# Experts of a mixture: outputs turned back later, rows turned earlier, biases copied first

## The reference

```python
x = x + gnn(layernorm(x), adj, adj, ...)     # two products with adj matrices per batch, gates, relu
x = x + ffn(layernorm(x), Wg, bg, W1, b1, W2, b2)

def ffn(x, Wg, bg, W1, b1, W2, b2):          # D = 128, H = 512, E = 8
    gate_logits = xf @ Wg + bg
    top_w, top_i = jax.lax.top_k(gate_logits, 2)
    w_dense = sum(one_hot(top_i, E) * softmax(top_w)[..., None], axis=1)
    for e in range(E):
        h = gelu(xf @ W1[e] + b1[e])
        out = out + w_dense[:, e:e+1] * (h @ W2[e] + b2[e])
```

## Time and profile before

| what | us |
|---|---|
| median of 3 runs (lowest, highest) | 772.68 (769.83, 773.42) |
| the profiled execution | 766.71 |
| its span, first to last instruction | 764.9 |
| PE busy | 689.8 |
| DVE busy | 625.5 |
| ACT busy | 515.6 |
| POOL busy | 501.9 |

### The profile page before, as it was taken

One profiled execution on the slowest core, in us unless ns is written; L12 is line 12 of the kernel. 1 busy time (PEld: TensorE's weight loads), 2 busy tenths in 40 slices (PEclk: granted clock), 3 DMA queues, 4 the chain that ended last, 5 costly groups with the idle time before them and its releaser, 6 DMA issues.

```text
span 764.9 us, 18892 instructions
## 1 busy us (share of the span) xinstructions
PE 689.8 (90%) x5004; PEld 627.9 (82%) x5004; DVE 625.5 (82%) x2129; ACT 515.6 (67%) x1389; POOL 501.9 (66%) x460
## 2 busy tenths in 40 slices
PE   3879999799997549999998999999999999999991
PEld 2557677577675439999998999998999999999990
DVE  5989986889989648888888788887888888888881
ACT  3888878478875326676776677776677777777770
POOL 1534656365665774655678578886888888888883
PEclk9997977578887559999999999999999999999996
DMA  8465878463522266578857867459764543544310
GB/s 255 145 203 159 287 261 97 80 140 106 208 92 76 98 189 187 180 216 285 254 169 242 258 176 192 129 173 359 225 170 127 140 126 99 152 124 126 86 43 15
DMA packets 100336, 127.07 MB, mean 166 GB/s; under 512 B 37367, under 2 KB 61824, under 8 KB 100240
## 3 DMA queue, kind: packets, MB, share of 16 engines
q1 hardware_dynamic: 81600, 83.41, 39.4%
q0 software_dynamic: 17344, 42.51, 16.6%
q10 hardware_dynamic: 1296, 0.14, 0.2%
HBM read 71.41 MB, written 56.99 MB: 168 GB/s over the span
## 4 chain that ended last, share of the span: by engine, by line
PE 50%; DMA 4%; issue 1%; POOL 1%; SPq 0%; POOLq 0%; DVE 0%
PE bank L1262 7%; PE bank L1264 7%; PE bank L1263 7%; PE bank L1276 7%; PE bank L1277 7%; PE bank L1281 7%; DMA w_t<-w_split 4%; PE bank L1290 3%; PE bank L1252 3%; POOL out_dram L645 1%; SPq L482 0%; POOLq L151 0%; SPq L466 0%; DVE row L1137 0%; SPq L476 0%
## 5 line engine op out<-in xcount | busy, mean ns | idle before, releaser
L767 ACT ACTIVATE act_f<-bank,b_t 128x256 f32<-128x256 f32 x560 | 220.0, 476 | 42.6 <-PE bank L1264 41.8
L645 POOL DMA_INDIRECT out_dram<-row,to_row x140 | 182.0, 1300 | 47.6 <-issue 36.3
L648 POOL DMA_INDIRECT rows<-row,to_row x140 | 162.5, 1160 | 76.5 <-DVE row L1137 46.7
L610 POOL DMA_INDIRECT rows<-row,slot_low x128 | 131.3, 1026 | 93.2 <-DVE row L833 58.1
L1125 DVE TENSOR_TENSOR act_lo<-act_f,act_hi 128x1024 fp32r<-128x1024 f32 x140 | 170.3, 1216 | 0.1
L1262 PE MATMUL bank<-in_hi,w_t 128*128 128x256 f32 x560 | 158.1, 282 | 4.0 <-DMA w_t<-w_split 4.0
L1264 PE MATMUL bank<-in_hi,w_t 128*128 128x256 f32 x560 | 157.3, 281 | 0.0
L1263 PE MATMUL bank<-in_lo,w_t 128*128 128x256 f32 x560 | 156.8, 280 | 0.0
L1276 PE MATMUL bank<-act_hi,w_t 128*128 128x256 f32 x560 | 149.6, 301 | 1.5 <-DMA w_t<-w_split 1.3
L1277 PE MATMUL bank<-act_hi,w_t 128*128 128x256 f32 x560 | 137.5, 280 | 0.0
L775 ACT ACTIVATE y_t<-bank,b_t 128x256 f32<-128x256 f32 x140 | 66.7, 476 | 99.8 <-PE bank L1281 99.8
(11 more groups left out here) (173 smaller groups left out, 1239.3 us busy)
## 6 DMA issues: line engine op xcount, KB each, us to landing
row<-rows SPq DMA_DIRECT2D x140, 260.0 KB, 2.9
w_t<-w_split SPq DMA_DIRECT2D x40, 512.0 KB, 5.2
xs<-in_x_dram SPq DMA_DIRECT2D x16, 512.0 KB, 4.4
rows<-ends_rep SPq DMA_DIRECT2D x14, 260.0 KB, 5.1
b_t<-biases SPq DMA_DIRECT2D x140, 2.5 KB
rows<-row,to_row POOLq DMA_INDIRECT x140
out_dram<-row,to_row POOLq DMA_INDIRECT x140
row<-in_L_ffn_W_dram SPq DMA_DIRECT2D x4, 512.0 KB, 9.7
```

Source lines behind the costliest of these rows:

```text
L610: pool.indirect_dma_start(out=rows, out_offset=bass.IndirectOffsetOnAxis(ap=slot_low[:, r, b:b + 1], axis=0), in_=row[:, r, b, :], in_offs ...
L645: pool.indirect_dma_start(out=out_rows, out_offset=at, in_=got[:, g, j, P:2 * P], in_offset=None, bounds_check=TOKENS - 1, oob_is_err=Fals ...
L648: pool.indirect_dma_start(out=rows, out_offset=at, in_=got[:, g, j, :], in_offset=None, bounds_check=NROWS - 1, oob_is_err=False).then_inc ...
L767: last = act.activation(act_f[:, s, c, :], ps_h[s][:, c, :], ACT.Gelu, bias=b_t[:, w, c:c + 1])
```

## The change

- PE, ACT, DVE and POOL write all 140 units out, without loops. The two passes no longer overlap on them: each pass begins its turned rows after the last outputs of the one before.
- Outputs are turned back four units behind (`BACK`), rows three units ahead (`IN`). PE: `layer1(t)`, `unit_back(t-4)`, `layer2(t-1)`, `unit_turned(t+3)`. ACT: `gelu(t)`, `copy_y(t-2)`, `tile_hi(t+3)`. DVE: `sum_up(t-5)`, `tile_lo(t+2)`, `hidden_hi(t)`, `hidden_lo(t)`. `in_hi`, `in_lo` get three slots, `y_t` four.
- Banks: halves of `ps_h` go round three banks, `ps_x` and `ps_o` take turns in three others, `ps_y` keeps two. `gelu` frees each half by itself.
- Biases: `b1` is copied behind the last weight load, ahead of the load of chunk 4, and `b2` behind the stores of the first four low parts.
- `row` has five slots, so L861 of chunk c waits for the scatter of chunk c-5. The last four chunks have semaphores of their own, and POOL counts them in `s_land`, which SP waits for.
- The second pass may use the table's counts for its first 12 units instead of 8.

```diff
-    EARLY = 2 * AHEAD
+    EARLY = [2 * AHEAD, 3 * AHEAD]
+    IN, BACK = 3, 4
+    LATE = 1
+    RING = 5
+    def of_pass(p):
+        return range(p * NU, (p + 1) * NU)
+    def bank_of_outputs(k):
+        return 5 + 2 * (k + BACK) % 3
+    def bank_of_rows(k):
+        return 5 + (2 * (k - IN) + 1) % 3
...
-        row = sb("row", [P, 4, G, ROW])
+        row = sb("row", [P, RING, G, ROW])
...
-        got = row[:].rearrange("p r (s j) k -> p (r s) j k", j=BLK)
+        got = row[:, 1:5].rearrange("p r (s j) k -> p (r s) j k", j=BLK)
...
-        for held in (row[:, 2], row[:, 3]):
+        for held in (row[:, 3], row[:, 4]):
...
+        def ps_h(t, half):
+            return bank[:, (2 * t.index + half) % 3, :].rearrange("p (c m) -> p c m", m=TILE)
+        def ps_y(t):
+            return bank[:, 3 + t.slot(2), 0:TILE]
...
             for k in range(4, E):
                 load_w(k)
+            biases(0, E)
 
             load_x(chunk_of(4))
             for k in range(4):
                 store_lo(k)
+            with nc.allow_non_contiguous_dma(reason="biases, once"):
+                sp.dma_start(b_dram[:, :, FC], b2).then_inc(s_bias, 16)
             load_x(chunk_of(5))
...
-            load_x(chunk_of(10))
-            biases(0, E // 2)
-            load_x(chunk_of(11))
-            biases(E // 2, E)
-            with nc.allow_non_contiguous_dma(reason="biases, once"):
-                sp.dma_start(b_dram[:, :, FC], b2).then_inc(s_bias, 16)
-            for k in range(12, CHUNKS):
+            for k in range(10, CHUNKS):
                 load_x(chunk_of(k))
...
                 def ready(k):
-                    if k % AHEAD == 0:
-                        sp.wait_ge(s_row[k // AHEAD], 16 * G * CHUNKS // 4)
-                    for i in range(k // AHEAD + 1, 4):
-                        sp.wait_ge(s_row[i], least[k] & 1023)
+                    if k == AHEAD:
+                        sp.wait_ge(s_land, 2)
+                    sp.wait_ge(s_land, least[k] & 7)
...
-            for k in range(CHUNKS):
+            for k in range(CHUNKS + 1):
                 scatter_rows(Turn(k // UA, k % UA, UA, CHUNKS))
+                if k > PART:
+                    pool.wait_ge(s_late[k - 1 - PART], 16 * G)
+                    pool.sem_inc(s_land, 1)
...
+            for p in range(PASSES):
+                units = of_pass(p)
+                for k in units[:IN]:
+                    tile_hi(unit(k))
+                for k in units:
+                    gelu(unit(k))
+                    if k - LATE - 1 in units:
+                        copy_y(unit(k - LATE - 1))
+                    if k + IN in units:
+                        tile_hi(unit(k + IN))
+                for k in units[-LATE - 1:]:
+                    copy_y(unit(k))
...
-                    wait_slot(dve, s_row, 16 * G, two, 0)
+                    left = two.index - RING
+                    if left >= 0:
+                        dve.wait_ge(s_row[left % 4], 16 * G * (left // 4 + 1))
...
+            for p in range(PASSES):
+                units = of_pass(p)
+                for k in units[:IN - 1]:
+                    tile_lo(unit(k))
+                for k in units:
+                    if k - BACK - 1 in units:
+                        sum_up(unit(k - BACK - 1))
+                    if k + IN - 1 in units:
+                        tile_lo(unit(k + IN - 1))
+                    hidden_hi(unit(k))
+                    hidden_lo(unit(k))
+                for k in units[-BACK - 1:]:
+                    sum_up(unit(k))
...
             def unit_turned(t):
+                units = of_pass(t.index // NU)
+                if t.index - IN in units:
+                    wait_turn(pe, s_done, 1, t, -IN - BACK if t.index - IN - BACK > units[0] else units[0] - t.index)
+                elif units[0] > 0:
+                    outputs = [k for k in range(units[0]) if bank_of_outputs(k) == bank_of_rows(t.index)]
+                    pe.wait_ge(s_done, outputs[-1] + 1)
...
             def unit_back(t):
+                if t.index + BACK + 1 in of_pass(t.index // NU):
+                    wait_turn(pe, s_inlo, 1, t.on(BACK + 1), 1)
+                else:
+                    wait_turn(pe, s_done, 1, t, -2)
...
             pe.wait_ge(s_slot, CHUNKS)
+            for p in range(PASSES):
+                units = of_pass(p)
+                for k in units[:IN]:
+                    unit_turned(unit(k))
+                for k in units:
+                    layer1(unit(k))
+                    if k - BACK in units:
+                        unit_back(unit(k - BACK))
+                    if k - LATE in units:
+                        layer2(unit(k - LATE))
+                    if k + IN in units:
+                        unit_turned(unit(k + IN))
+                for k in units[-BACK:-LATE]:
+                    unit_back(unit(k))
+                for k in units[-LATE:]:
+                    layer2(unit(k))
+                for k in units[-LATE:]:
+                    unit_back(unit(k))
```

More of the change, by code:

```diff
@@ L65, in wait_slot @@
     wait_turn(eng, sems[s], each, Turn(turn.group, (turn.step - s) // ring, turn.unroll // ring, 0), more)
[L68 to L91, removed]
 class Own:
@@ L228, in program @@
         new = sb("new", [P, PASSES])
[L229 removed]
+        unit_at_ = sb("unit", [P, 6, 2, PASSES])
         code = sb("code", [P, 32])
@@ L1061, in _ @@
             own.sync()
-            first, rows_of, seg, lim, at, start = (unit[:, i] for i in range(6))
+            first, rows_of, seg, lim, at, start = (unit_at_[:, i] for i in range(6))
             own(dve.scalar_tensor_tensor(out=change[:], in0=expert[:, 2], scalar=1.0, in1=expert[:, 0], op0=ALU.max, op1=ALU.not_equal))
@@ L1155, in _, with sum_up @@
-            for k in range(UNIT_SPANS[1][1] * UT, UNITS):
-                step(unit_at(k), 1)
-            for k in range(UNITS - 2, UNITS):
-                sum_up(unit_at(k), 1)
+                dve.tensor_tensor(act_lo[:, s], act_f[:, t.slot(2)], act_hi[:, s].bitcast(F32), ALU.subtract).then_inc(s_hlo, 1)
+            def sum_up(t):
+                g, second = t.slot(GR), int(t.index >= NU)
+                wait_turn(dve, s_o, 1, t, 1)
+                at = TOKEN_AT if second else NEXT_AT
+                dve.scalar_tensor_tensor(out=to_row[:, g, :], in0=skip[:, t.index, :], scalar=BIG, in1=got_i[:, g, :, at],
+                                         op0=ALU.mult, op1=ALU.max)
+                for j in range(BLK):
+                    w = got[:, g, j, W_AT + second:W_AT + second + 1]
+                    last = dve.scalar_tensor_tensor(out=got[:, g, j, P:2 * P], in0=ps_o(t)[:, j, :], scalar=w,
+                                                    in1=got[:, g, j, P:2 * P], op0=ALU.mult, op1=ALU.add)
+                last.then_inc(s_done, 1)
@@ L1284, in unit_back @@
-            def unit_back(t):
-                if t.real:
-                    wait_turn(pe, s_y, 1, t, 1)
-                    wait_turn(pe, s_done, 1, t, 0)
-                    s = t.slot(2)
-                    for j in range(BLK):
-                        last = pe.transpose(ps_o[:, j, :], y_t[:, s, j * P:(j + 1) * P], ident[:])
-                    last.then_inc(s_o, 1)
-            def step(t):
-                layer1(t)
-                unit_back(t.back(2))
-                unit_turned(t.on(2))
-                layer2(t.back(1))
@@ new lines, in layer2 @@
+            def layer2(t):
+                s, w = t.slot(LATE + 1), t.slot(WR)
+                wait_slot(pe, s_w2, 16, t, 16)
+                wait_turn(pe, s_hhi, 1, t, 1)
+                wait_turn(pe, s_y, 1, t, -1)
+                for c in range(FC):
+                    hi, lo = (w2_t[:, w, k, c * P:(c + 1) * P] for k in range(2))
+                    pe.matmul(ps_y(t), hi, act_hi[:, s, c, :], start=(c == 0), stop=False)
+                    pe.matmul(ps_y(t), lo, act_hi[:, s, c, :], start=False, stop=False)
+                wait_turn(pe, s_hlo, 1, t, 1)
+                for c in range(FC):
+                    hi = w2_t[:, w, 0, c * P:(c + 1) * P]
+                    last = pe.matmul(ps_y(t), hi, act_lo[:, s, c, :], start=False, stop=(c == FC - 1))
+                last.then_inc(s_mm2, 1)
```

240 lines of the change are left out of this document (91 added, 149 removed).

## The result

| what | before | after |
|---|---|---|
| median of the runs, us (lowest, highest) | 771.25 (768.44, 773.42) | 782.46 (777.28, 783.72) |
| ratio, 95% interval | | 1.0135 (1.0075 to 1.0194) |
| the profiled execution, us | 766.71 | 783.72 |
| its span, us | 764.9 | 781.7 |
| PE, DVE, POOL busy, us | 689.8, 625.5, 501.9 | 695.1, 635.0, 487.3 |

The change made the kernel slower by 11 us; 782 was forecast. Measured again in ten runs beside 25 of the kernel before (771.08), the changed kernel stood at 778.99 us, ratio 1.0079 (1.0041 to 1.0118). The two intervals share 0.75% to 1.18%, so the loss is about 1%, some 8 us. The second profile of after spans 774.5 us, 9.6 more than before's.

A forecast was written before the change was run, and what follows sets the result against it. PE was taken to bound the expert stage, DVE to be busiest in the chunk stage. Expert stage +10.9 and chunk stage -0.7 give +10.2 on the profiled 766.7; plus 6.0, 782 us, range 776 to 787.

The forecast's parts named there:

- The end: After the last first layer: five outputs still open, POOL's scatters end at 761.1 instead of 755.5, +5.6 us.
- The boundary: Between the passes: first layer of unit 70 comes 6.35 us later, some 0.5 given back, +5.9, bounds 3.8 and 6.5.
- The middle: Units inside a pass: moving the turns apart changes nothing, 0, bounds 0 to 1.4 us in all.
- The start: First units of the expert stage: the 1.1 us wait of L1252 behind DVE goes, -0.6 us.
- Turn 10: Chunk stage: the 8.60 us scatter wait at L861 goes, less 0.9 for other waits, -7.7 us.
- Chunk 4's x: Chunk stage: early bias writes hold back the load of chunk 4 and DVE waits, +8.0 us, bounds 1 and 11.
- rival A: Chunk stage: the bias copies fit into the DMA engines' idle gap, 774.9 us in all; chance 0.16.
- Five slots: Chunk stage: the six small scatter waits at L861 shrink by about 1.0 us, bounds 0 and -4.8.
- The 6.0 us added from profile to median: Whole kernel: median of the runs before stood 6.0 us above the profiled execution, unexplained, so 6.0 was added.
- Rival B: Chunk stage: timed runs lose their extra 6.0 us in scatter waits; these and all 13.4 go, 764.2 us; chance 0.12.
- POOL, unit of 3.07: Expert stage: scatters starting inside DVE's cast make POOL's unit 3.07 us, below 3.25, so POOL holds its pace.
- rival C: POOL is locked out longer and ends 2.5 us later, bias writes at their slow end, +3: 788 us; chance 0.08.

The follow-up runs named there:

- e6: The changed kernel with outputs turned back three units behind instead of four, passes still emptied: 779.18 us, 1.0104 of the kernel before.
- e11: The changed kernel with its two passes joined and outputs turned back three units behind instead of four: 772.13 us, 1.000 of the kernel before.
- e5b: The changed kernel with its two passes joined, without emptying between them, outputs still four units behind: 781.46 us, 1.0116 of the kernel before.
- e3b: The kernel before with five row slots instead of four, nothing else: 762.66 us in four runs, 0.9851 of the kernel before.
- e0: The changed kernel itself, measured again in ten runs: 778.99 us, 1.0079 of the kernel before.

## Why the prediction was right

- **The end, +5.6:** measured +5.3 and +5.4 in two profiles. The mechanism, five units that POOL works through at two scatters of 1.28, is shown by e6 and e11, where one unit less of distance ends 2.56 sooner.
- **The boundary, +6.35 and -0.5 given back:** the interval came at +6.2, with PE's wait of 1.73 where the working had 1.6. Given back was 0.2, and in the second profile nothing (+1.0). The number is right for the drained kernel. What the prediction had not seen is that the emptying is only one of two things that cost this time. It followed PE's, ACT's and DVE's orders over the boundary, and not SP's wait for the landed count: when the passes are joined at distance four that wait takes the drain's place (e5b, +7.9), and when the distance is three but the passes are emptied the drain stays (e6, +7.0). Only both together help (e11, +3.4). The 1.66 of the lower bound has no working in the prediction; four pairs of 0.22 and twelve matmuls at 0.12 make 2.3, which would put that bound at 3.3. It decided nothing.
- **The middle, 0:** +0.010 a unit, 1.4 us, at the bound. Weight waits, for which I allowed 0 to 2, came at 7.7 us in the first profile and 5.4 in the second, against 5.5 before (I had read the 1.5 at L1276 as a few tenths). So units 0 to 69 gave +2.3 in one profile and -1.2 in the other.
- **The start, -0.6:** wrong, it is +2.1 in both profiles (+1.0 to +2.3 in the other four with the changed order). The turns of the three first units' rows, before the first layer:

```profile
280.52 0.66 PE L1253 MATMUL bank<-ident,row 128*128 128x128 f32 x2 [3.59 <-DMA row<-rows]
282.07 0.69 PE L1253 MATMUL bank<-ident,row 128*128 128x128 f32 x2 [0.89 <-DMA row<-rows]
283.65 0.69 PE L1253 MATMUL bank<-ident,row 128*128 128x128 f32 x2 [0.88 <-DVE in_lo L1117]
```

Unit 1's turn comes 1.5 us behind unit 0's, held by its rows' load, and unit 2's turn waits for DVE's low part; both now stand ahead of the first layer, which starts at 284.0. From unit 0's turn to the first layer that is 3.5 us, where before needs 2.1 (278.76 to 280.85). I had taken the wait of DVE as removed, and it was only put in another place, with a load's before it. The other 0.7 lies ahead of unit 0's turn, and e3b, with before's expert stage, has 0.8 of the same (37.3 us).
- **Turn 10, -7.7:** -7.9 and -8.3.
- **Chunk 4's x, +8.0:** the wait was 8.57 and the turn +8.9, in e0 4.9 and +7.4; over the five profiles with early biases beside before's 771 the turn was 19.5 to 24.1 us, so a spread of 4.6 us lies on this term alone. The prediction had the copies through by about 50 us, and the last landed at 50.9 (49.4 in e0, 54.3 in e6). The second batch was the right row for this, and rival A's idle gap was too short by far: 4096 writes need some 25 us. Read as 6.2 ns a write, though, the price holds for a queue with other traffic beside it; the stores of the weights, which the prediction does not mention, are part of it here.
- **Five slots, -1.0:** the 13 turns without a long wait gave +0.3 and -2.8 in the two profiles, on both sides of it. That waits at L887 (L891 in after) take the place of those at L861 is shown: their `issue` row grew from 8.6 to 15.0 and 12.3 us. What I had not asked is what five slots do where the biases stay late: they take 5.1 us off before's chunk stage (e3b), more than the whole change does (+1.3 and -3.8).
- **The 6.0 us added from profile to median:** the weakest term. In the first measurement the changed kernel's runs stand 1.3 below the profiled execution, 783.72, and that execution is 6.8 above the sum's 776.9. In the second the profiled execution took 776.55, 0.35 under the sum, and the runs stood 2.4 above it. So the 6.0 of the kernel before did not carry over to the changed one, and that 782 was met so closely by 782.46 is luck: in the first profile the span grew by 16.8 us instead of 10.2, and the 6.0 made up for it. (And 782.9 rounds to 783.) Held against e0, where the span grew by 9.6, the forecast is 3 us too high, which is this term. The terms of the boundary, the end, turn 10 and chunk 4 are the prediction's merit, the last digit of the sum is not.
- **Rival B** (the extra time of before's runs sits in its scatter waits): it did not come, as its condition, bias copies that fit into the gap, failed. e3b takes away all 13.4 us of these waits and wins 8.4 of the 19.4 that the rival counted on; 6.1 us came back at `t_sum`, which is what the prediction had against it.
- **POOL, unit of 3.07:** it holds in after, as the last section shows, and rival C with it falls away: POOL keeps step with DVE.

The fastest version measured beside a kernel before at 771 us is e3b, five row slots and nothing else, with 762.66 us in four runs; beside one at 856 us the same kernel gained nothing.

## What to carry to other kernels

Where a pipeline reads back what it has written, the distance at which outputs are handled costs once at the end and again at each point of reading back. Emptying the pipeline there and waiting for the landed data are two stops for the same stretch of time: taking one away uncovers the other, so look for what stands behind a stop before pricing its removal, in the queue that issues the loads too. Lengthen distances only to remove a wait that the profile shows.

Judge the parts of a combined change one at a time. Here the fifth slot was worth some 5 us of the chunk stage and was buried under 11 to 14 us of an expert stage that had little wait to lose.

Thousands of four-byte writes in one lump hold the load behind them in the queue back, here 4096 of them, with the stores of the weights beside the load's last part, by some 14 us (it landed at 51 instead of 37); ask first which load stands behind them. And a constant that is added from a profile to a median, without a cause, is no part of a forecast: put it into the range.

## What the runs showed of the hardware

**A scatter of POOL that begins inside a cast of DVE is 0.46 to 0.49 us longer.** POOL and DVE's cast in the second pass, before:

```profile
600.77 1.17 POOL L645 DMA_INDIRECT out_dram<-row,to_row  x1 [0.30 <-issue]
602.17 0.69 DVE L1120 CAST act_hi<-act_f 128x1024 fp32r<-128x1024 f32 x1
602.25 1.47 POOL L645 DMA_INDIRECT out_dram<-row,to_row  x1 [0.30 <-issue]
```

After, in the second pass and at the end of the first:

```profile
600.47 0.69 DVE L1122 CAST act_hi<-act_f 128x1024 fp32r<-128x1024 f32 x1 [0.36 <-ACT act_f L769]
600.57 1.44 POOL L653 DMA_INDIRECT out_dram<-row,to_row  x1 [0.53 <-issue]
602.32 0.98 POOL L653 DMA_INDIRECT out_dram<-row,to_row  x1 [0.30 <-issue]
...
517.87 1.21 POOL L656 DMA_INDIRECT rows<-row,to_row  x1 [0.53 <-issue]
519.38 0.98 POOL L656 DMA_INDIRECT rows<-row,to_row  x1 [0.30 <-issue]
520.89 1.21 POOL L656 DMA_INDIRECT rows<-row,to_row  x1 [0.53 <-issue]
```

A scatter with nothing beside it takes 0.98 and 0.30 of gap (the rows of the end). One that begins 0.08 to 0.10 after the start of a cast, when some 0.6 of the cast are left, takes 1.44 to 1.48. One that begins 0.34 after it (517.87, the cast from 517.53) takes 1.21. So the delay is what is left of the cast, less 0.12. The rule of the Trainium skill (SBUF — State Buffer, Who interferes with whom) is that a two-port cast locks GpSimd out for its whole length. The rows agree as far as they go, for the time from the scatter's start; they show no delay of the full 0.69.

In after POOL waits for DVE in nearly every unit. Its first scatter starts some 0.8 after the end of DVE's `sum_up`, with a gap of 0.53, and does so at 759.72 too, where no cast is near. So the gap is not the cast's, POOL's own need is 1.44 + 0.98 + 2 x 0.30 = 3.02 us a unit, close to the prediction's 3.07, and at the end of the first pass, where units come 3.02 apart, POOL keeps step with them.

In before the other scatter of a unit takes 1.17, and from its start to its end (600.77 to 601.94) DVE runs no cast. With this 0.19 a unit comes to 3.24 us, and POOL doesn't catch up: its scatters end 6.2 us behind DVE through the second pass, in e3b 4.7, and e3b's tail is 1.3 shorter for it. Where the 0.19 comes from stays open.

**Small writes starve the queue.** Between 28 and 40 us the engines are 0.14 busy at 2 GB/s, and still the load behind, issued at 35.8, is not let through; undisturbed it took 3.7 us. The time is not in the engines' busy share; a low share there is no free room.
